# Attention scores of a two-layer block: the high part and the rest of queries and keys stacked along the 128 rows of one float32r product

## The reference

```python
q = (x @ wq).reshape(Bq, Tq, N_KV, N_REP, HEAD_DIM)      # 2 groups of 4 heads, 128 wide
k_lat = (x @ wk_down).reshape(Bq, Tq, N_KV, D_LAT)       # 32 wide, one for each group
k = jnp.einsum('bkhl,ld->bkhd', k_lat, wk_up)
scores = jnp.einsum('bqhrd,bkhd->bhrqk', q, k) * scale
scores = jnp.where(causal, scores, jnp.finfo(scores.dtype).min)
probs = jax.nn.softmax(scores, axis=-1)
```

## Time and profile before

| | |
|---|---|
| median of three runs | 1374.36 us (1373.46 to 1374.67) |
| span of the profiled execution | 1379.8 us |
| its own time, beside the span | none is given but the span, which is 5.4 us above the median |
| PE busy | 1207.2 us, 87% of the span |
| DVE busy | 1037.0 us, 75% |
| ACT busy | 852.2 us, 62% |
| POOL busy | 489.3 us, 35% |
| DMA | 53.22 MB in 18514 packets |

### The profile page before, as it was taken

How to read it: one execution, slowest core, us unless ns; L and a number is a source line. 1 busy time by engine, 2 the same in 40 slices (tenths; PEclk the granted TensorE clock), 3 DMA queues, 4 the chain that set the end, 5 groups by cost and what they waited for, 6 DMA issues and landing times. The chain is left out here.

```text
span 1379.8 us, 19465 instructions
## 1 busy us (share of the span) xinstructions
PE 1207.2 (87%) x6560; PEld 760.5 (55%) x6560; DVE 1037.0 (75%) x2381; ACT 852.2 (62%) x1600; POOL 489.3 (35%) x309
## 2 busy tenths in 40 slices
PE   5974689989998889989999889989899899889698
PEld 3651145655665556555656456655656556555456
DVE  3666977599866997589866997579975998569822
ACT  2634446488646966489565866479664876469332
POOL 0103930078002950069100960049300870029300
PEclk8995579999999999999999999999999999999899
DMA  7101100030001200020001200021000300011000
GB/s 245 70 16 64 60 8 1 16 108 16 16 17 55 69 12 6 16 92 31 17 9 43 88 1 17 16 78 47 16 1 16 109 16 9 1 64 60 8 1 8
DMA packets 18514, 53.22 MB, mean 39 GB/s; under 512 B 4976, under 2 KB 5864, under 8 KB 18032
## 3 DMA queue, kind: packets, MB, share of 16 engines
q1 hardware_dynamic: 16112, 43.40, 9.8%
q0 software_dynamic: 1296, 4.20, 1.0%
q10 hardware_dynamic: 1008, 4.38, 0.8%
HBM read 45.40 MB, written 2.38 MB: 35 GB/s over the span
## 5 line engine op out<-in xcount | busy, mean ns | idle before, releaser
L1482 DVE TENSOR_TENSOR_SCAN probs_T<-bank,probs_T 128x512 f32<-128x512 f32 x256 | 303.9, 1212 | 16.1 <-ACT bank L1078 12.1
L618 PEld LDWEIGHTS bank<-w_w,hidden 128*128 128x128 f32 x2048 | 248.8, 192 | 72.9 <-issue 66.8
L602 PE MATMUL bank<-hT,w_w 128*128 128x512 f32 x512 | 262.9, 629 | 27.1 <-ACT hidden L933 26.2
L447 POOL TENSOR_TENSOR probs_T<-step_space,probs_T 128x1024 f32<-128x1024 f32 x120 | 282.2, 2358 | 5.9 <-DVE probs_T L1482 5.7
L618 PE MATMUL bank<-w_w,hidden 128*128 128x128 f32 x2048 | 251.6, 276 | 2.1 <-DVE expert_sum L1174 1.6
L933 ACT ACTIVATE hidden<-bank,w_b 128x512 f32<-128x512 f32 x256 | 169.6, 686 | 117.5 <-PE bank L602 116.9
L1006 ACT ACTIVATE probs<-bank,row_neg 128x128 f32<-128x128 f32 (+3 forms) x256 | 134.8, 528 | 151.7 <-DVE row_neg L1335 134.8
L1078 ACT ACTIVATE bank<-step_space,a_neg 128x512 f32<-128x512 f32 x256 | 167.8, 683 | 55.0 <-DVE probs_T L1482 36.7
L701 PE MATMUL bank<-k_pad,q_lat 128*128 128x512 f32 (+3 forms) x512 | 185.3, 448 | 5.8 <-DMA k_pad<-xc 5.8
L1335 DVE TENSOR_REDUCE row_neg<-bank 128x1 f32<-128x128 f32 (+3 forms) x256 | 123.5, 487 | 85.1 <-PE bank L703 82.7
L602 PEld LDWEIGHTS bank<-hT,w_w 128*128 128x128 f32 x512 | 89.0, 194 | 153.0 <-ACT hidden L933 97.0
(11 more groups left out here) (183 smaller groups left out, 1577.6 us busy)
## 6 DMA issues: line engine op xcount, KB each, us to landing
probs_T<-b_rows_dram SPq DMA_DIRECT2D x64, 512.0 KB, 3.7
w_w<-in_w_dram ACTq DMA_DIRECT2D x2, 2048.0 KB, 14.0
k_pad<-xc SPq DMA_DIRECT2D x64, 64.0 KB, 2.0
x_in<-in_x_dram POOLq DMA_DIRECT2D x8, 256.0 KB, 3.3
gate<-gate_rows_dram SPq DMA_DIRECT2D x1, 2048.0 KB, 7.0
out_dram<-x_out POOLq DMA_DIRECT2D x7, 256.0 KB, 2.8
step_space<-in_wmod_dram SPq DMA_DIRECT2D x1, 768.0 KB, 5.6
probs_T<-in_wqT_dram SPq DMA_DIRECT2D x1, 512.0 KB, 4.1
```

The lines of the kernel that those rows point to most:

```text
L447: ins = nc.gpsimd.tensor_tensor(inject[:, n % 3, :, :], u[:], row.unsqueeze(1).to_broadcast([P, DH, T]), ALU.mult)
L602: mm(hid1_bank(n)[:], w["w1"][:, n // C1, n % C1 * P:(n % C1 + 1) * P], hT[3][:], start=True, stop=True).then_inc(hid1_mm.sem, 1)
L618: ins = mm(to[:, t * P:(t + 1) * P], hidden[:, (e * C1 + c) % (2 * C1), t * P:(t + 1) * P], w["w2"][:, e * C1 + c, :], start=(c == 0), sto ...
L1482: v.tensor_tensor_scan(state[:, n % 2, c, :], decay(DH * n + c)[:], inject[:, n % 3, c, :], 0.0, ALU.mult, ALU.add).then_inc(st_ok.sem, 1)
```

## The change

Each query and key is split into a high part, its value rounded to float32r by a copy, and the rest, the float32 value less the high part (again as float32r). The four cross products of high part and rest are laid along the 128 rows: `q_terms` holds for each of 8 heads the rows high, rest, high, rest (4 x 32), `k_terms` for each of 2 groups the rows high, high, rest, rest. One float32r product over 128 rows then sums all four. Zero-padded keys are gone.

The copies of the high parts are on DVE (`split_heads`), the two subtractions on POOL (`split_rest`), and SP places the queries with 32 DMAs of 64 KB a batch in place of 8 for the keys (`place_queries`). `k_terms` needs no DMA, since the key projection already has four copies of the keys along the partitions. The high part and the rest of the queries lie in `probs` until they are placed, so the scan of the batch before waits for `q_placed` ahead of its first read. In the first batch queries are projected ahead of keys.

```diff
 F32 = mybir.dt.float32
+F32R = mybir.dt.float32r
 BF16 = mybir.dt.bfloat16
...
 FAR = -3.0e38
+TERMS = 4
...
         q_lat = sb("q_lat", [P, G, T])
-        k_pad = sb("k_pad", [P, G, HG, T])
+        q_terms = sb("q_terms", [P, H, T], F32R)
+        k_terms = sb("k_terms", [P, G, T], F32R)
         v_lat = sb("v_lat", [P, NT, G * L])
         row_neg = sb("row_neg", [P, 4])
         probs = sb("probs", [P, 2, 2, T])
+        q_hi, q_lo = probs[:, 0, :, :], probs[:, 1, :, :]
         probs_ring = probs[:].rearrange("p a b k -> p (a b) k")
...
         weights_in, experts_in = sem("weights_in"), sem("experts_in")
-        pad_zero = sem("pad_zero")
         first_in = sem("first_in")
...
         k_lat = signal("k_lat", G)
-        k_out = signal("k_out", 16 * G * HG)
+        q_split = signal("q_split", 1)
+        k_split = signal("k_split", 1)
+        q_rest = signal("q_rest", 1)
+        k_rest = signal("k_rest", 1)
+        q_placed = signal("q_placed", 16 * TERMS * H)
         v_mm = signal("v_mm", 1)
...
         def _(sp):
-            def place_keys(b):
-                for g in range(G):
-                    sp.wait_ge(k_lat.sem, k_lat.at(b, g + 1))
-                    if g == 0:
-                        sp.wait_ge(pad_zero, 1)
-                    for j in range(HG):
-                        sp.dma_start(k_pad[j * L:(j + 1) * L, g, j, :], k_four[j * L:(j + 1) * L, g, :]
-                                     ).then_inc(k_out.sem, 16)
+            def place_queries(b):
+                for half, source in enumerate((q_hi, q_lo)):
+                    if half == 0:
+                        sp.wait_ge(q_split.sem, q_split.at(b, 1))
+                    else:
+                        sp.wait_ge(q_rest.sem, q_rest.at(b, 1))
+                    for g in range(G):
+                        for j in range(HG):
+                            for r in range(half, TERMS, 2):
+                                sp.dma_start(q_terms[r * L:(r + 1) * L, g * HG + j, :].bitcast(F32), source[j * L:(j + 1) * L, g, :]
+                                             ).then_inc(q_placed.sem, 16)
...
                 sp.dma_start(w[name][:], io[name]).then_inc(weights_in, 16)
-            place_keys(0)
+            place_queries(0)
             sp.wait_ge(setup_gate, 4)
...
             for b in range(0, B - 1):
-                place_keys(b + 1)
+                place_queries(b + 1)
                 spread_rows(b)
...
+            def split_rest(b):
+                pool.wait_ge(q_split.sem, q_split.at(b, 1))
+                nc.gpsimd.tensor_tensor(q_lo.bitcast(F32R), q_lat[:], q_hi, ALU.subtract).then_inc(q_rest.sem, 1)
+                pool.wait_ge(k_split.sem, k_split.at(b, 1))
+                pool.wait_ge(q_rest.sem, q_rest.at(b, 1))
+                nc.gpsimd.tensor_tensor(k_terms[2 * L:, :, :], k_four[2 * L:, :, :], k_terms[2 * L:, :, :].bitcast(F32),
+                                        ALU.subtract).then_inc(k_rest.sem, 1)
+                pool.wait_ge(k_rest.sem, k_rest.at(b, 1))
             def gate_weights(b):
...
                     gate_proj(b + 1)
+                    pool.wait_ge(weights_gated.sem, weights_gated.at(b + 1, PROJ))
+                    split_rest(b + 1)
                     pool.wait_ge(bias_added.sem, bias_added.at(b, 1))
...
             load(0, True)
+            split_rest(0)
             load(1)
...
                 if k < 4:
-                    mm(to[:], w["wk4"][:, k, :] if k < 2 else w_qk[:, k - 2, :], hT[0][:], start=True, stop=True
+                    mm(to[:], w_qk[:, k, :] if k < 2 else w["wk4"][:, k - 2, :], hT[0][:], start=True, stop=True
                        ).then_inc(q_mm.sem, 1)
...
                     if n == 0:
-                        pe.wait_ge(k_out.sem, k_out.at(b, 16 * G * HG))
+                        pe.wait_ge(q_placed.sem, q_placed.at(b, 16 * TERMS * H))
+                        pe.wait_ge(k_rest.sem, k_rest.at(b, 1))
                         pe.wait_ge(v_out.sem, v_out.at(b, 1))
...
                     s = bank[SCORE_BANK[n % 4]]
-                    mm(s[:, 0:(i + 1) * P], q_lat[:, g, i * P:(i + 1) * P], k_pad[:, g, j, 0:(i + 1) * P],
+                    mm(s[:, 0:(i + 1) * P], q_terms[:, g * HG + j, i * P:(i + 1) * P], k_terms[:, g, 0:(i + 1) * P],
                        start=True, stop=False)
...
                 if ahead:
-                    act.wait_ge(k_out.sem, k_out.at(b + 1, 16 * G * HG))
+                    act.wait_ge(k_rest.sem, k_rest.at(b + 1, 1))
                 for c in range(DH):
...
                 act.wait_ge(q_mm.sem, q_mm.at(0, g + 1))
-                f(k_four[:, g, :], bank[FIRST_BANK[g]][:], ACT.Copy).then_inc(k_lat.sem, 1)
+                f(q_lat[:, g, :], bank[FIRST_BANK[g]][:], ACT.Copy).then_inc(q_out.sem, 1)
             for g in range(G):
                 act.wait_ge(q_mm.sem, q_mm.at(0, G + g + 1))
-                f(q_lat[:, g, :], bank[FIRST_BANK[G + g]][:], ACT.Copy).then_inc(q_out.sem, 1)
+                f(k_four[:, g, :], bank[FIRST_BANK[G + g]][:], ACT.Copy).then_inc(k_lat.sem, 1)
             act.wait_ge(v_mm.sem, v_mm.at(0, 1))
...
             v.memset(xi[:], 0.0)
-            v.memset(k_pad[:], 0.0).then_inc(pad_zero, 1)
             dve.wait_ge(first_in, 16 * n_first)
...
                     ts(a_neg[:], a_exp[:], -1.0, None, ALU.mult).then_inc(setup_v, 1)
+            def split_heads(b):
+                dve.wait_ge(q_out.sem, q_out.at(b, G))
+                cp(q_hi.bitcast(F32R), q_lat[:]).then_inc(q_split.sem, 1)
+                dve.wait_ge(k_lat.sem, k_lat.at(b, G))
+                cp(k_terms[:], k_four[:]).then_inc(k_split.sem, 1)
...
                 ln_normalise(b, 2, x, mark, link)
+                if b < B - 1:
+                    split_heads(b + 1)
                 early(0)
...
                             read_product(b, n - 1)
+                    if n == 0 and b < B - 1:
+                        dve.wait_ge(q_placed.sem, q_placed.at(b + 1, 16 * TERMS * H))
                     if n in SCAN_ADD:
...
             first_modulation()
+            split_heads(0)
             attend(0, False, True, False)
```

## The result

The changed kernel takes 1389.18 us (median of four runs, 1388.01 to 1389.53), the kernel before, on the same chip, 1374.17 (1373.46 to 1374.67): a ratio of 1.010, 95% interval 1.0083 to 1.0118. It is 15 us slower, where 1378 was forecast in a range of 1356 to 1402.

What follows compares the result with a forecast made beforehand. PE was taken as the fullest engine, DVE close behind and the next bound. Terms +15.2 + 8.4 + 1.9 - 5 - 16.8 = +3.7 us on the median 1374.36 gave 1378; range 1356 to 1402, the forecast's own 1367 to 1389.

Steps and rivals of the forecast that it cites:

- Start: Start of the run: 24 more DMA issues on SP at 0.634 us delay the first scores by 15.2 us.
- rival 2: SP's DMA queue: new DMAs issue 0.36 us apart, 32 take 11.5 us; time 1359 us; chance 0.10.
- Score product: On PE: a float32r column costs 0.43 ns, not 1.58, so PE loses 11.8 us a batch.
- Rival 4: Score product on PE: float32r costs four passes, so no gain; time 1400 us; chance 0.11.
- PE near 26 us: Sign of a right forecast: PE's busy time in batch 3's attention falls from 38.0 to 26.2 us.
- Path gain of batches 1 to 7: Attentions: all DVE waits for scores but the two longest go, 2.4 us a batch, 16.8 in all.
- rival 5: Later attentions: PE's clock falls to 0.50; three attentions of seven would give 1418 us; chance 0.05.
- Batch 0: First batch: attention gains 5 us (bounds 0 and 16.6); its third scan can run 1.9 us later.
- Copies and subtractions: Two DVE copies of 0.8 us and two POOL subtractions of 2.36 us a batch fit idle time, free.
- Scans of batches 1 to 6: B rows' save 4.7 us late on SP; scans 3.1 late, 1.7 taken back: +1.4 a batch, 8.4 for six.
- rival 3: Scans: SP's lateness goes through, every batch loses the 4.7 us; time 1401 us; chance 0.12.
- The offset: Whole run: profiled execution spans 1379.8 us, 5.4 above the median 1374.36; the summed difference was added to the median, giving 1378.

Runs made afterwards that it cites:

- the fast product alone: Kernel before with queries and padded keys made float32r, without the rests or any added DMA, copy or subtraction; 1360.88 us, ratio 0.9854.

## Why the prediction was right, and where it was wrong

The direction was right (slower had 0.48, the most), and so was the reason: SP's list of DMAs costs more than the faster product gives. The size was not: +3.7 us forecast, +15.0 measured, which the range took in and the forecast's own range of 1367 to 1389 just missed. That narrower range does not come out of its terms either: a gain of 1.5 to 3.5 for 2.4 in seven batches and one us either way in six make 1364 to 1390. Step by step:

- **Start: right.** +15.2 forecast, +14.9 measured. 24 more issues at 0.634 us, nothing beside them; rival 2 (cheap issues) falls, since a new issue took 591 ns.
- **Score product: right.** 0.43 ns a column was taken; the doubled products show 0.44. Rival 4 falls. But PE's busy time fell by 9.6 us in the attention of batch 3 and by 8.7 a batch on average, for 11.8 forecast: "PE near 26 us" became 28.4.
- **Path gain of batches 1 to 7: right in sum, short of a cause.** 16.8 forecast, 16.8 measured, DVE the bound and the two longest waits left, as said. That the sum agrees so closely is luck: by the row maxima the gain is 3.2 us for batches 3 and 6, whose clock stayed at 1.00, 1.0 to 1.7 for 2, 4 and 5, where it fell, 1.8 for 7, and 4.5 for 1, whose attention before had run in part at the low level. The falls are rival 5 in a small form. It was priced as whole attentions at 0.50; what came was stretches of a few us, right behind idle time of PE. The Trainium skill, "TensorE: Matmul & The Clock Gate", "A second HAM failure mode: psum-queue depth-cycling", tells of another kernel, in which short idle times between groups of products make the clock alternate between its two levels. The trace agrees in that the clock fell behind such idle times; what it cost is the 2.3 us between the two attentions shown above.
- **Batch 0: mis-sized.** 5 forecast for the attention, 8.2 measured, within the bounds of 0 and 16.6. The reason for taking little, that the clock "will stay there longer" at 0.50, did not come true: it stood there until 9.3 us after the first score product, before until 12.2 us after. +1.9 forecast for its scan's start, +1.2 measured.
- **Copies and subtractions: free, as forecast.** The scans are on time in the version with 16 DMAs, which has all of them. The casts took 0.69 us each for 0.8; the subtraction on 64 partitions took 2.61, above the 2.36 that was to bound it. They are not alone, though: gating took 2.25 us on POOL beside DVE's casts, 1.27 before.
- **Scans of batches 1 to 6: the step that failed among the terms.** "+1.4 x 6 = 8.4" became 26.4 - 9.5 = 16.9. The chain was the right one, each link a little short: 32 issues took 20.7 to 21.8 us for 20.3, so the save stood 5.0 to 6.1 us behind its projection for 4.7; the first spread followed after 1.83 us for 1.58 and landed after 3.7 to 4.3 for 3.7. The first scan came 4.4 us late on average, for 3.1. The scans took back 9.5 / 6 = 1.6 us, near the 1.7 forecast, but for another reason than "these wait for PE, which the B rows do not touch" says: of these waits, what exceeds the 58.84 us of an undisturbed scan comes from the clock at the scan's start, and an execution without that fall has only 58.84 - 58.00 = 0.84 us to take back, which makes +3.6 a batch against such an execution. To that, rival 3 (4.7 a batch) lay nearer than the forecast; to the 2.8 between the two profiles, the forecast did.
- **The offset: the larger error.** The terms sum to +6.4 in the profiles for +3.7 forecast, 2.7 us off; the forecast was 11 off. The rest is "I add the difference to the median". In the runs here a time is 1.8 us above its span, so the profiled execution of before stood 7.2 us above its median, while that of the changed kernel stood 1.2 below its own. Part of these 7.2 us are clock falls at the starts of scans (4.4 us over batches 1 to 6; gone when PE is kept busy); the changed kernel's scans fall too but hide it behind their lateness. So part of the gain that the sum booked against that execution was probably not there against the median. Shown are the falls and their cost: the second profile of the kernel before is 2.3 us shorter, and its scans of batches 1 to 6 are 2.6 us shorter. Not shown is that the executions near the median had fewer falls, for none of them was profiled; and this kernel's median itself was 1374 to 1379 us in the three comparisons. What else made that execution long stays open.

## What to carry to other kernels

Count a change's DMAs by issues on the queue that carries them and ask what is queued behind: 24 more issues cost 15 us at the start and 4.4 us of lateness a batch, and one slice that takes two groups at once (16 issues for 32) turned a loss of 15 us into a gain of 14.5. When PE gets faster under another bound, look at the granted clock stretch by stretch, for its new idle time may be paid back at half speed just behind it. Before a stall of one profile is booked as a reserve, see whether it stands in every batch with the same length: 58.84 us four times and 59.8 twice says that it isn't the program's.

## What the runs showed of the hardware that was not expected

- Unread products keep the clock up: with 1.89 us of them in an idle time of 2.3 us, all scans of batches 1 to 6 in the three kernels that had them, 18 of 18, took 58.84 or 58.85 us at a clock of 1.00. Without them the clock fell at the start of 22 of 30 (five profiles whose scans began on time).
- Two queues that copied within SBUF at the same time, at the one place where it was tried, were slower than one: 0.83 and 0.92 us an issue against 0.66, landing 4.1 us against 3.0. The Trainium skill, "DMA: Bandwidth & Descriptors", "Issuing engines are not separate DMA queues", says that issuing from several engines saves only the time of issuing. Here even that was mostly lost.
- A DVE product of 32 columns took 0.77 us for 0.18 and ended with the POOL subtraction beside it. The Trainium skill, "SBUF — State Buffer", "SBUF: two separate sides", has the two engines share a pair of ports that one holds for a whole instruction. The trace agrees, with POOL's instruction from 556.18 to 558.54 and DVE's from 557.83 to 558.60.
- Batch 0 took 57.8, 54.3 and 53.3 us between attention and scan at a granted clock of 0.77, 0.88 and 0.91 (the kernel before, the same kept busy in later batches, the fast product alone), with the same program in this stretch. Why the clock differs there is not shown.
